# Storing a bf16 part once with a repeating source, and ordering the rows in DRAM by dimension

## The chip, the cores and the metric

The kernel runs on one core of a Trainium2 chip. The metric is the device time of one execution in microseconds (us). A core has TensorE (PE, matrix products and transposes), VectorE (DVE), ScalarE (ACT), GpSimd (POOL) and SyncE (SP, which here only issues DMAs), and 16 DMA engines that move data between DRAM and the on-chip memory.

## The reference, cut to what matters

The input x is 8 batches of 512 rows of 128 numbers. Four layers follow one another, each adding to x: attention a (its weights are sigmoids of sums of sines), a mixture-of-experts layer, attention b (softmax with a relative position term), and the experts again. What the change touches are the two attention layers:

```
x = x + attn_a(layernorm(x));  x = x + ffn(layernorm(x))
x = x + attn_b(layernorm(x));  x = x + ffn(layernorm(x))

q = (x @ Wq.T + bq)   k = (x @ Wk.T + bk)   v = (x @ Wv.T + bv)     # 16 heads of 8 numbers
attn_a: sim = q k / sqrt(8) / temp;  w = sigmoid(sum_f alpha * sin(2 pi sim / freq + phi)); normalised; w v
attn_b: scores = q k / sqrt(8) + q pos + k pos;  softmax;  probs v
```

The products q k are computed from bf16 numbers and must be nearly as exact as in float32. So every q and k is split into three bf16 parts, high (h), middle (m) and low (l), with q = h + m + l. Six of the nine products of a part of q with a part of k are kept.

## The kernel before, in words

The work runs as blocks, one after the other; a block starts when every engine has finished the one before. In order: `project_block("a")`, `wave_attention`, `wave_output`, `layer_norm`, `experts`, `project_block("b")`, `distance_attention`, `layer_norm`, `experts`, `last_block`.

**project_block** (from L160) loops over the 8 batches. DVE normalises x for the batch two ahead (`normalise`, L338); TensorE transposes it (L508); ACT copies it out of PSUM (L464); TensorE makes q, v and k (L518, L520, L522); ACT adds the bias and writes `full` (L472, L477) and its bf16 high part (L481); DVE subtracts that to get `rest` (L359, in layer a after the largest absolute value, L357); ACT casts `rest` to the middle part (L485); DVE subtracts again and writes the low part (L368). All parts are held in two buffers, by the parity of the batch. A part is a tile of 128 partitions (16 heads of 8 dimensions) by 512 rows of x. DVE also adds the bias to v (L347); in layer b the result lies in `Vs`, again two buffers.

SP sends the parts to DRAM in `send(b)`, in program order: for q and then for k it goes through the six letters of LEFT = "hhmhlm" or RIGHT = "hmhlhm" and issues one DMA of 128 KB for each, so each part is stored as many times as its letter stands there. That gives 12 DMAs for a batch; layer b has a 13th, `v_b` (L269). In DRAM the six rows of eight dimensions form NR = 48 rows: row r * 8 + d is part r of dimension d. Matching rows of q and k hold the six kept products, so one matrix product over 48 rows gives q k. In layer a an array is (batch and head, 48, 512) and a DMA writes runs of 1 KB. In layer b it is (48, 4, batch and head, 128): the 512 rows cut into four tiles, and a DMA writes runs of 256 bytes. The same is done once for the position table, `t_parts`, from 8 partitions (L295).

Three kinds of wait tie the engines to the stores: the buffer of a part is written again only when the stores of two batches before have landed (`stored`, in front of L481 and L368), and `Vs` only when `v_b` has (`v_stored`, in front of L347). At the end of the block SP waits for all stores. In layer a, GpSimd ends its part with a maximum over all partitions of the largest values that DVE found (L405, then L448, then L450).

**wave_attention** loads 48 rows of four heads for each group of four heads (L597), runs of 1 KB. Its inner loop is untouched.

**distance_attention** (from L1511) works on two batches (32 heads) at a time. The unit is a pair of a q tile and a k tile of 128 rows; 16 units make a group, there are four groups. `load` (L1678 to L1682) brings one tile of 32 heads into 48 partitions, twice, at partitions 0 and 64 (`ODD`), 384 KB each; in DRAM the 32 heads of a row are 8 KB without a gap. `ks` has three buffers and `qs` two. A k tile is loaded when the last content product (L1808) of the unit that used its buffer is done, a q tile after the last unit of the q tile two before. GpSimd then spreads each loaded tile with four copies of about 2 us (`spread`, L1735) into `kb` or `qb`, and TensorE's position products (L1795) read these in halves. SP, GpSimd, TensorE, ACT and DVE each follow a fixed order that is worked out ahead (`plan`, `dve_plan`, `spread_steps`).

Of the kernel before, what the change touches and what calls it, by code (L numbers as in the profile page):

```python
# [8 lines left out]
BF16 = mybir.dt.bfloat16  # L9
# [6 lines left out]
P = 128  # L16
B, L, D = 8, 512, 128
H, HD = 16, 8
# [16 lines left out]
ACT_LAST = (0,)  # L35


LEFT = "hhmhlm"
RIGHT = "hmhlhm"
NR = len(LEFT) * HD  # L40
ODD = 64
FRAC = 24
# [5 lines left out]
def build(nc, a):  # L48
    ctx = ExitStack()
    with ctx:  # L50
        dram = {
            n: nc.dram_tensor(n, (B * H, NR, L), BF16, kind="Internal").ap()
            for n in ("qa_parts", "ka_parts")
        }
        for n in ("qb_parts", "kb_parts"):
            dram[n] = nc.dram_tensor(n, (NR, QT, B * H, P), BF16, kind="Internal").ap()
        dram["xn"] = nc.dram_tensor("xn", (NT * P, D), F32, kind="Internal").ap()
        dram["ys"] = nc.dram_tensor("ys", (TILES * P, D), F32, kind="Internal").ap()
        dram["t_parts"] = nc.dram_tensor("t_parts", (NR, 2, WIN), BF16, kind="Internal").ap()
# [100 lines left out]
def project_block(nc, sb, ps, sem, layer, a, X, V, ident, mv, rstd, dram, params, bound):  # L160
# [10 lines left out]
    with ExitStack() as c:  # L171
# [64 lines left out]
        t_stored = sem(c, layer + "_t_stored")  # L236
        block = c.enter_context(nc.Block())
        nload = 6 + (3 if wave else 0)
        each = 16 * len(LEFT)

        @block.sync
        def _(sp):
            x = a["x"].rearrange("b (t p) d -> b p t d", p=P)

            def load_x(b):
                sp.dma_start(X[:, b * QT:(b + 1) * QT, :], x[b]).then_inc(x_loaded[b], 16)

            def send(b):
                u = b % 2
                for s, (_, dst, order) in enumerate(sides):  # L250
                    for r, w in enumerate(order):
                        if r == 0:
                            sp.wait_ge(high, b * NS + s + 1)
                        if w == "l":
                            sp.wait_ge(low, b * NS + s + 1)
                        if w == "m":
                            sp.wait_ge(mid, b * NS + s + 1)
                        if wave:
                            sp.dma_start(
                                dram[dst][b * H:(b + 1) * H, r * HD:(r + 1) * HD, :],  # L260
                                part[s, w][:, u, :]).then_inc(stored[s][u], 16)
                        else:
                            sp.dma_start(
                                dram[dst][r * HD:(r + 1) * HD, :, b * H:(b + 1) * H, :]
                                .rearrange("d t h n -> h d t n"),
                                part[s, w][:, u, :].rearrange("p (t n) -> p t n", t=QT)).then_inc(stored[s][u], 16)
                if not wave:
                    sp.wait_ge(v_taken, (b + 1) * QT)
                    sp.dma_start(dram["v_b"][b, :, :],  # L269
                                 Vs[:, u].rearrange("p g t h d -> p (g t h d)")).then_inc(v_stored[u], 16)  # L270

            if wave:
                load_x(0)
                load_x(1)
                sp.dma_start(temp[:, 0:1], a["temperature"].to_broadcast((P, 1))).then_inc(small, 16)
                sp.dma_start(raw[:, 0, :], a["phi"].to_broadcast((P, H * NF))).then_inc(small, 16)
                sp.dma_start(raw[:, 1, :], a["alpha"].to_broadcast((P, H * NF))).then_inc(small, 16)
            for t, src in ((wq, "wq"), (wk, "wk"), (wv, "wv")):
                sp.dma_start(t[:], a[layer + "_" + src]).then_inc(small, 16)
            for t, src in ((bq, "bq"), (bk, "bk")):  # L280
                sp.dma_start(t[:], a[layer + "_" + src]).then_inc(small, 16)
            sp.dma_start(bv[:], a[layer + "_bv"].to_broadcast((P, D))).then_inc(small, 16)
            if wave:
                for b in range(2, B):
                    load_x(b)
                sp.wait_ge(t_clear, 1)
                sp.dma_start(t_full[:, 0, 0:WIN - 1], a["table_up"]).then_inc(t_loaded, 16)
                sp.dma_start(t_full[:, 1, 0:WIN - 1], a["table_down"]).then_inc(t_loaded, 16)
            for b in range(B):
                send(b)  # L290
                if wave and b == B - 2:
                    sp.wait_ge(t_step, 6)
                    for way, order in enumerate((LEFT, RIGHT)):
                        for r, w in enumerate(order):
                            sp.dma_start(dram["t_parts"][r * HD:(r + 1) * HD, way, :],  # L295
                                         t_part[w][:, way, :]).then_inc(t_stored, 16)
            for u in range(2):
                if not wave:
                    sp.wait_ge(v_stored[u], 16 * (B // 2))
                for s in range(NS):  # L300
                    sp.wait_ge(stored[s][u], each * (B // 2))
            if wave:
                sp.wait_ge(t_stored, 32 * len(LEFT))

        @block.vector
        def _(dve):
# [1204 lines left out]
def distance_attention(nc, sb, ps, sem, a, X, ident, dram):  # L1511
# [125 lines left out]
    with ExitStack() as c:  # L1637
# [38 lines left out]
        def _(sp):  # L1676

            def load(dst, src, q, t, landed):  # L1678
                g = q // QT
                for at in (0, ODD):  # L1680
                    sp.dma_start(dst[at:at + NR, :, :],
                                 dram[src][:, t, g * BH:(g + 1) * BH, :]).then_inc(landed, 16)  # L1682

            def load_q(q):
                if q >= 2:
# [327 lines left out]
```

## Time and profile before

| what | value |
|---|---|
| time, median of 3 runs | 4173.84 us (4168.84 to 4179.46) |
| the profiled execution: its own time, its span | 4163.56 us, 4161.8 us |
| project_block a | starts with the program, ends about 113 us |
| wave_attention | about 113 to 2082 us |
| project_block b | about 2521 to 2610 us |
| distance_attention | about 2611 to 3754 us for its loads, to about 3830 in all |
| share of the span: PE, DVE, ACT, POOL | 82%, 83%, 69%, 27% |
| mean share of the 16 DMA engines by queue 1 (SP's DMAs) | 12.3% |

The shares of busy time are means over blocks of very different kinds. The change touches two short blocks and the loads of a long one, so a stretch has to be read by itself.

### The profile page before, as it was taken

To read this page: it belongs to the slowest core of one execution; us is meant where nothing else is said; L and a number is where in the kernel's file an instruction comes from. 1 tells how busy PE (TensorE), PEld (TensorE's weight loads), DVE (VectorE), ACT (ScalarE), POOL (GpSimd) and SP (SyncE) were. 2 spreads that over 40 slices of the span, in tenths; PEclk is the share of its full clock that TensorE was granted. 3 is DMA by queue.
4 is the path that set the end of the run, shared out by engine and by line. 5 is a ranking of instruction groups with operands and counts; after the bars stand their busy time and mean duration, and the time that the engine had idled before them with its cause. 6 is when DMAs were issued, how large, how long until landed. Compare 5 with 4: busy or idle time off the path is not lost. (4 is left out here: it accounts for less than half of the span.)

```text
span 4161.8 us, 71345 instructions
## 1 busy us (share of the span) xinstructions
PE 3403.4 (82%) x27092; PEld 2090.7 (50%) x27092; DVE 3438.3 (83%) x4264; ACT 2880.8 (69%) x2433; POOL 1126.6 (27%) x983
## 2 busy tenths in 40 slices
PE   3799999999999999999938933688988888897990
PEld 2233333333333333333336932587887887887790
DVE  7899999999999999999847634678788787787662
ACT  3799999999999999999804313466665666664530
POOL 2111221121121112112101541535334335321235
PEclk8899999999999999999967966799999999998995
DMA  4100000000000000000032226411202102102122
GB/s 132 30 6 13 13 13 6 13 13 10 9 13 13 6 13 13 13 6 13 5 106 72 68 52 138 81 25 32 45 18 47 31 17 47 30 18 64 34 65 66
DMA packets 145098, 146.44 MB, mean 35 GB/s; under 512 B 62673, under 2 KB 123697, under 8 KB 140113
## 3 DMA queue, kind: packets, MB, share of 16 engines
q1 hardware_dynamic: 136144, 125.04, 12.3%
q0 software_dynamic: 8704, 17.84, 1.8%
q8 instruction: 186, 3.05, 0.3%
q14 instruction: 64, 0.52, 0.0%
HBM read 90.73 MB, written 52.10 MB: 34 GB/s over the span
## 5 line engine op out<-in xcount | busy, mean ns | idle before, releaser
L704 PE MATMUL psA<-wave,diag 128*128 128x512 f32 x3072 | 1433.9, 618 | 138.2 <-DVE score L860 86.7
L772 ACT ACTIVATE wave<-wave 128x2048 f32<-128x2048 int32 x640 | 1180.8, 1904 | 3.3 <-DVE wave L847 2.2
L704 PEld LDWEIGHTS psA<-wave,diag 128*128 128x128 f32 x3072 | 579.8, 195 | 893.2 <-issue 693.6
L641 POOL TENSOR_TENSOR diag<-ident,par 128x128 f32<-128x128 f32 x384 | 298.1, 803 | 1431.2 <-PE psA L704 1431.2
L822 DVE TENSOR_SCALAR wave<-s,par 128x2048 int32<-128x2048 int32 x480 | 610.6, 1272 | 0.0
L847 DVE TENSOR_SCALAR wave<-wave 128x2048 int32<-128x2048 int32 x512 | 608.0, 1211 | 0.0
L1735 POOL COPY kb<-ks 48x1024 bf16<-48x1024 bf16 x160 | 330.7, 2067 | 590.3 <-PE psR L1795 421.9
L1876 ACT COPY r<-psR 128x1024 f32<-128x1024 f32 x320 | 310.7, 1025 | 163.0 <-PE psR L1795 163.0
L737 ACT ACTIVATE s<-psS,par 128x1024 int32<-128x1024 f32 x256 | 282.8, 1105 | 128.8 <-PE psS L667 128.8
L1885 ACT ACTIVATE W<-psR 128x1024 f32<-128x1024 f32 x256 | 253.4, 1025 | 167.7 <-PE psR L1820 164.8
L860 DVE SCALAR_TENSOR_TENSOR score<-wave,par,psA 128x1024 f32<-128x1024 f32 x256 | 317.2, 1268 | 35.0 <-PE psA L704 35.0
L1915 DVE TENSOR_TENSOR S<-psR,S 128x1024 f32<-128x1024 f32 x192 | 234.6, 1222 | 112.9 <-PE psR L1811 112.9
L1930 DVE TENSOR_TENSOR S<-S,m 128x1024 f32<-128x1024 f32 x256 | 324.7, 1319 | 0.6
L860 DVE SCALAR_TENSOR_TENSOR score<-wave,par,score 128x1024 f32<-128x1024 f32 x256 | 316.1, 1272 | 0.0
L1820 PE MATMUL psR<-ident,S 128*128 128x128 f32 x2048 | 263.3, 279 | 53.7 <-DVE S L1930 52.5
L1922 DVE TENSOR_REDUCE mx<-S 128x8 f32<-128x1024 f32 x256 | 303.8, 1213 | 1.7
L1811 PE MATMUL psR<-ident,r 128*128 128x128 f32 x2048 | 282.4, 284 | 0.0
L1876 ACT COPY S<-psR 128x1024 f32<-128x1024 f32 x192 | 188.4, 1018 | 131.5 <-PE psR L1795 131.5
L1820 PEld LDWEIGHTS psR<-ident,S 128*128 128x128 f32 x2048 | 226.5, 142 | 77.1 <-DVE S L1930 71.7
L679 PE MATMUL psO<-score,Vg 128*9 128x512 f32 x1056 | 239.8, 596 | 7.8 <-ACT score L754 7.8
L754 ACT ACTIVATE score<-score 128x2048 f32<-128x2048 f32 x132 | 241.4, 1900 | 6.1 <-DVE score L860 5.7
L1811 PEld LDWEIGHTS psR<-ident,r 128*128 128x128 f32 x2048 | 232.8, 146 | 0.0
(259 smaller groups left out, 4444.0 us busy)
## 6 DMA issues: line engine op xcount, KB each, us to landing
ks<-kb_parts SPq DMA_DIRECT2D x56, 384.0 KB, 6.2
qs<-qb_parts SPq DMA_DIRECT2D x32, 384.0 KB, 6.2
ys<-f_ys SPq DMA_DIRECT2D x36, 256.0 KB, 2.5
wave_out<-og SPq DMA_DIRECT2D x33, 256.0 KB, 2.1
o<-wave_out SPq DMA_DIRECT2D x8, 1024.0 KB, 5.2
qp<-qa_parts SPq DMA_DIRECT2D x32, 192.0 KB, 3.5
kp<-ka_parts SPq DMA_DIRECT2D x32, 192.0 KB, 3.9
f_wu<-in_w_up SPq DMA_DIRECT2D x2, 2048.0 KB, 10.3
```

The lines of the kernel that those rows point to most:

```text
L641: ins = pool.tensor_tensor(diag[:, h % 2, f, :], ident[:], par[:, u, 1, h * NF + f:h * NF + f + 1] .to_broadcast((P, P)), ALU.mult)
L704: mm = pe.matmul(psA[:, kt, :], diag[:, h % 2, f, :], wave[:, h % 2, f, kt * L:(kt + 1) * L], start=(f == 0), stop=(f == PE_F - 1), skip_g ...
L772: act.activation(wave[:, h % 2, f, :], angle[:, h % 2, f, :], ACT.Sin, scale=float(TWO_PI / 2.0 ** 32)).then_inc(sine, 1)
L822: dve.tensor_scalar(angle[:, h % 2, f, :], src, scalar, par[:, u, row, h * NF + f:h * NF + f + 1], ALU.mult, ALU.add).then_inc(turned if f ...
L847: dve.tensor_scalar(angle[:, h % 2, f - 1, :], at, 32 - FRAC, None, ALU.logical_shift_left).then_inc(cut, 1)
L860: dve.scalar_tensor_tensor(out=score[:, u * HG + h, cols], in0=wave[:, h % 2, f, cols], scalar=par[:, u, 1, h * NF + f:h * NF + f + 1], in ...
L1735: pool.tensor_copy(dst[rows, pairs, odd, :], src[rows, :, :].rearrange("r h (n two) -> r n h two", two=2)[:, pairs, :, odd]).then_inc(read ...
L1811: mm = pe.matmul(slot[:, j, :], r1[:, u % 2, k * HB + j, :], ident[:], start=False, stop=True, is_transpose=True, skip_group_check=True)
L1820: mm = pe.matmul(slot[:, i, kt * P:(kt + 1) * P], S[:, 2 * j + i, kt * P:(kt + 1) * P], ident[:], start=(kt == 0), stop=True, is_transpose ...
L1876: act.copy(dst[:, :, k * CP:(k + 1) * CP], psR[:, n % RING, :, :].rearrange("p a (n h) -> p h (a n)", h=BH)).then_inc(act_took, 1)
L1922: dve.tensor_reduce(mx[:, hs, kt], S[:, hs, kt * P:(kt + 1) * P], AX.X, ALU.max).then_inc(maxed, 1)
L1930: dve.tensor_tensor(S[:, hs, :], S[:, hs, :], m[:, hs].rearrange("p (h a) -> p h a", a=1).to_broadcast((P, 2, L)), ALU.subtract).then_inc( ...
```

## The change

Each part is stored once, by a DMA whose source repeats the part (a step of 0 over `count` copies), into all of its rows. For that the six letters are put in another order (LEFT "hhhmml", RIGHT "mhlhmh"; the same six pairs hh, hm, hl, mh, mm, lh), so that the rows of one letter have a constant step, and a row in DRAM is now d * 6 + r. `PLACES` gives for each letter its first row, step and count. A batch has 6 stores in place of 12, of 3, 2 and 1 copies (384, 256 and 128 KB); the bytes are the same. Layer b uses the layout of layer a, (batch and head, 48, 512); its stores write runs of 1 KB, and `load` in distance_attention gathers runs of 256 bytes: 48 rows of 32 heads, 1536 runs where there were 48 of 8 KB.

```diff
-LEFT = "hhmhlm"
-RIGHT = "hmhlhm"
+LEFT = "hhhmml"
+RIGHT = "mhlhmh"
+
+PLACES = {LEFT: (("h", 0, 1, 3), ("m", 3, 1, 2), ("l", 5, 1, 1)), RIGHT: (("h", 1, 2, 3), ("m", 0, 4, 2), ("l", 2, 1, 1))}
...
-            for n in ("qa_parts", "ka_parts")
+            for n in ("qa_parts", "ka_parts", "qb_parts", "kb_parts")
         }
-        for n in ("qb_parts", "kb_parts"):
-            dram[n] = nc.dram_tensor(n, (NR, QT, B * H, P), BF16, kind="Internal").ap()
...
-        each = 16 * len(LEFT)
+        each = 16 * len(PLACES[LEFT])
...
-                    for r, w in enumerate(order):
-                        if r == 0:
-                            sp.wait_ge(high, b * NS + s + 1)
-                        if w == "l":
-                            sp.wait_ge(low, b * NS + s + 1)
-                        if w == "m":
-                            sp.wait_ge(mid, b * NS + s + 1)
-                        if wave:
-                            sp.dma_start(
-                                dram[dst][b * H:(b + 1) * H, r * HD:(r + 1) * HD, :],
-                                part[s, w][:, u, :]).then_inc(stored[s][u], 16)
-                        else:
-                            sp.dma_start(
-                                dram[dst][r * HD:(r + 1) * HD, :, b * H:(b + 1) * H, :]
-                                .rearrange("d t h n -> h d t n"),
-                                part[s, w][:, u, :].rearrange("p (t n) -> p t n", t=QT)).then_inc(stored[s][u], 16)
+                    for w, first, step, count in PLACES[order]:
+                        sp.wait_ge({"h": high, "m": mid, "l": low}[w], b * NS + s + 1)
+                        sp.dma_start(
+                            dram[dst][b * H:(b + 1) * H, :, :].rearrange("h (d r) n -> (h d) r n", d=HD)
+                            [:, first:first + step * (count - 1) + 1:step, :],
+                            part[s, w][:, u, :].rearrange("p (a n) -> p a n", a=1).to_broadcast((P, count, L))
+                        ).then_inc(stored[s][u], 16)
...
-                        for r, w in enumerate(order):
-                            sp.dma_start(dram["t_parts"][r * HD:(r + 1) * HD, way, :],
-                                         t_part[w][:, way, :]).then_inc(t_stored, 16)
+                        for w, first, step, count in PLACES[order]:
+                            sp.dma_start(
+                                dram["t_parts"][:, way, :].rearrange("(d r) n -> d r n", d=HD)
+                                [:, first:first + step * (count - 1) + 1:step, :],
+                                t_part[w][:, way, :].rearrange("p (a n) -> p a n", a=1).to_broadcast((HD, count, WIN))
+                            ).then_inc(t_stored, 16)
...
                     sp.dma_start(dst[at:at + NR, :, :],
-                                 dram[src][:, t, g * BH:(g + 1) * BH, :]).then_inc(landed, 16)
+                                 dram[src][g * BH:(g + 1) * BH, :, t * P:(t + 1) * P]
+                                 .rearrange("h r n -> r h n")).then_inc(landed, 16)
```

## Rows read from the trace of the kernel before

**Rows 1.** The page: busy us of each engine and its share of the span.

```profile
PE 3403.4 (82%) x27092; PEld 2090.7 (50%) x27092; DVE 3438.3 (83%) x4264; ACT 2880.8 (69%) x2433; POOL 1126.6 (27%) x983
```

**Rows 2.** Timeline of SP's issues, project_block a (start, us, instruction), and the next block's first.

```profile
45.31 0.60 SPq L259 DMA_DIRECT2D qa_parts<-a_part0h  x1
...
110.33 0.60 SPq L259 DMA_DIRECT2D ka_parts<-a_part1m  x1
...
113.27 0.35 SPq L597 DMA_DIRECT2D qp<-qa_parts  x1
```

**Rows 3.** Timeline, project_block a: DVE's normalise and low part, ACT's high part.

```profile
53.04 1.10 DVE L338 TENSOR_SCALAR a_xn<-X,mv,rstd 128x128 f32<-128x128 f32 x4
57.22 0.69 DVE L368 TENSOR_TENSOR a_part1l<-a_rest,a_part1m 128x512 bf16<-128x512 f32 x1
58.62 1.10 DVE L338 TENSOR_SCALAR a_xn<-X,mv,rstd 128x128 f32<-128x128 f32 x4
69.78 0.62 ACT L481 CAST a_part1h<-a_full 128x512 bf16<-128x512 f32 x1 [3.98 <-DMA ka_parts<-a_part1m]
```

**Rows 4.** Timeline, the end of project_block a on DVE and POOL.

```profile
95.70 0.69 DVE L368 TENSOR_TENSOR a_part1l<-a_rest,a_part1m 128x512 bf16<-128x512 f32 x1
103.82 0.18 POOL L450 TENSOR_TENSOR bound<-a_topa 128x1 f32<-128x1 f32 x1 [6.84 <-issue]
```

**Rows 5.** Busy time by stretch: PE, PEld, DVE, ACT, POOL, granted clock, DMA share, GB/s.

```profile
52.00:99.00 47.00, 23.11 (x77) 12.95 (x76) 33.83 (x90) 24.38 (x41) 0.37 (x1) 0.80 0.71 198
2546.00:2607.00 61.00, 22.95 (x80) 12.95 (x78) 24.45 (x64) 25.01 (x41) 0.00 (x0) 0.77 0.93 211
2719.00:2726.00 7.00, 5.34 (x131) 4.73 (x128) 3.35 (x3) 5.17 (x6) 0.00 (x0) 1.00 0.59 115
```

**Rows 6.** DMA rate (GB/s in 40 slices), 4153.9 to 4161.5 us: the output's store.

```profile
GB/s 0 0 0 0 0 143 339 348 348 345 350 345 348 345 350 348 353 348 348 350 350 348 345 348 348 345 348 345 353 353 348 348 350 348 350 345 345 116 0 0
```

**Rows 7.** Timeline of SP's issues: six loads of x, each 256 KB in 512 runs.

```profile
6.21 3.91 SPq L246 DMA_DIRECT2D X<-in_x  x6
```

**Rows 8.** Timeline of SP's issues, project_block b, and the next block's first.

```profile
2545.27 0.64 SPq L269 DMA_DIRECT2D v_b<-b_Vs  x1
...
2607.37 0.64 SPq L269 DMA_DIRECT2D v_b<-b_Vs  x1
2612.90 0.80 SPq L1681 DMA_DIRECT2D qs<-qb_parts  x2
```

**Rows 9.** Timeline of DVE, project_block b: a low part, and a later wait for a store.

```profile
2545.24 0.69 DVE L368 TENSOR_TENSOR b_part1l<-b_rest,b_part1m 128x512 bf16<-128x512 f32 x1
2557.02 0.88 DVE L347 TENSOR_TENSOR b_Vs<-b_psV,b_bv 128x128 f32<-128x128 f32 x4 [4.46 <-DMA v_b<-b_Vs]
```

**Rows 10.** The page's DMA issues: size of one, median us from issue to landing.

```profile
v_b<-b_Vs SPq DMA_DIRECT2D x8, 288.0 KB, 2.7
```

**Rows 11.** Timeline, the start of distance_attention: POOL's spreads, and TensorE after the second.

```profile
2619.90 7.82 POOL L1735 COPY qb<-qs 48x1024 bf16<-48x1024 bf16 x4 [5.77 <-DMA qs<-qb_parts]
2627.78 7.89 POOL L1735 COPY kb<-ks 48x1024 bf16<-48x1024 bf16 x4
2631.74 1.73 PEld L1795 LDWEIGHTS psR<-kb,T 112*128 112x128 bf16 x32 [2.09 <-POOL kb L1735]
```

**Rows 12.** Timeline, distance_attention: the spread after a load, the next one, and its reader.

```profile
2796.43 8.12 POOL L1735 COPY kb<-ks 48x1024 bf16<-48x1024 bf16 x4 [11.01 <-DMA ks<-kb_parts]
2810.56 8.24 POOL L1735 COPY qb<-qs 48x1024 bf16<-48x1024 bf16 x4 [6.00 <-PE psR L1795]
2819.86 1.09 PE L1795 MATMUL psR<-qb,T 112*128 112x64 bf16 x32 [0.60 <-DVE S L1915]
3561.22 8.26 POOL L1735 COPY qb<-qs 48x1024 bf16<-48x1024 bf16 x4 [2.19 <-PE psR L1795]
```

**Rows 13.** Timeline of TensorE after ACT's wait in project_block a: first and last product.

```profile
70.93 2.08 PE L518 MATMUL a_psQ<-a_xnT,a_wq 128*128 128x512 f32 x2 [4.64 <-ACT a_xnT L464]
...
74.50 1.92 PE L522 MATMUL a_psK<-a_xnT,a_wk 128*128 128x512 f32 x2
```

More of the change, by code:

```diff
@@ L302, in _ @@
             if wave:
-                sp.wait_ge(t_stored, 32 * len(LEFT))
+                sp.wait_ge(t_stored, 32 * len(PLACES[LEFT]))
         @block.vector
```

## Prediction

> **What bounds the kernel now.** The page's busy times come first [rows 1]: PE and DVE are each busy for four fifths of the span and POOL for a quarter, which says that no DMA bounds the kernel as a whole. The change touches two blocks of some 90 us and the loads of a third, so the rest is read stretch by stretch. The three long blocks (wave attention and the two expert layers) keep their work; only their starting times move.
>
> SP's issues in project_block a show the bound there. From 45.31 to 110.33 us [rows 2] SP issues 92 stores of parts and the 12 small ones of the position table almost without a gap: 0.60 us each, 0.65 from start to start, so a batch of 12 takes 7.8 us (and 92 x 0.65 + 12 x 0.34 = 63.9 of the 65.0 us). No engine is full there [rows 5]: DVE 33.8 of 47 us, PE 23.1, ACT 24.4, DMA 0.71. What the batches are paced by is SP's issuing. ACT then waits for a buffer whose stores haven't landed, 3.98 us in the worst case [rows 3]. Ahead of that, while buffers are free, DVE's `normalise` rows stand 5.58 us apart (53.04 and 58.62 [rows 3]): the pace that compute can keep.
>
> Project_block b is the same with 13 stores: its `v_b` rows stand at 2545.27 and 2607.37, seven batches apart, 8.87 us each [rows 8]. DVE waits 4.46 us for `v_b` to free `Vs` [rows 9], and the DMA engines are 0.93 busy at 211 GB/s [rows 5]: runs of 256 bytes make the engines nearly as full as SP.
>
> **Block a, part by part.** Six stores in place of 12. What does one cost to issue? Bounds: 0.33 us, a `v_b` that comes alone, is below anything seen in a stream; a store now takes 0.65. The six loads of x, each 512 runs over 128 partitions, take 3.91 us, 0.65 each [rows 7]. A repeating store has 128 to 384 runs over the same 128 partitions, so I take 0.65: six are 3.9 us, less than the 5.58 of compute. If issuing costs by the copy instead, 12 copies at 0.65, nothing is gained (a rival below).
>
> The bytes stay: 12 x 131,072 = 1.57 MB a batch. At the rate per busy time that the stream shows, 198 / 0.71 = 279 GB/s [rows 5], they take 5.64 us; at the 348 GB/s of the output's store, a full queue of short runs [rows 6], 4.5 us. Both are at or under compute. So compute sets the pace, 5.58 us a batch, and the position table's six stores saved (0.34 each in the timeline, 2 us) lie in SP's new slack.
>
> Then the end. The last low part of the third batch (b = 2) ends at 57.91 [rows 3]. Three batches at 5.58 bring b = 5 to 74.7. The last two don't normalise, 1.10 us less; I give them 5.0 each for what DVE waits, so 84.7. Now another thing is late: POOL's reduction. The last low part starts at 95.70 and `bound` is done at 104.00 [rows 4], 7.6 us after its end. Today SP is still issuing then, so it costs nothing; afterwards it sets the end: 84.7 + 7.6 = 92.3 us, while the last store lands about 2 + 2.4 us after 84.7. The next block's first row comes 0.5 us after the last landing today (110.33 + 2.4 = 112.7, then 113.27 [rows 2]), so it moves from 113.3 to 92.8: **20.5 us saved**.
>
> **Block b.** Seven issues at 0.65 are 4.6 us, and DVE's own work is 24.45 us in 61, or 3.6 for a batch of 8.87 [rows 5], 4.6 back to back. The bytes are 1.57 + 0.29 = 1.87 MB: 5.4 us at 348 GB/s, 6.7 at 279. A loop adds to it: `v_b` is the last of its batch to be issued and lands 2.7 us later [rows 10], and DVE can't take v two batches on before that. I take 6.0 us, between the two data rates and near the lower, since the queue will be full as it is in [rows 6]. The second batch's last low part ends at 2545.93 [rows 9]; six more batches give 2581.9. Behind it SP still issues three k stores and `v_b` (about 2.5 us), and that lands 2.7 later: 2587.1. Today the last `v_b` lands at 2607.37 + 2.7 = 2610.1 [rows 8]. **23 us saved**; with 5.4 us a batch it would be 26.6, with 6.7 us 18.8.
>
> **The loads of distance_attention.** No row shows a load of 256-byte runs. A pair (both places, 768 KB) keeps the engines busy for 0.59 x 7 = 4.1 us now [rows 5], 21 ns for each future run of 256 bytes if only bytes counted (3072 runs on 16 engines, 192 each). Stores of such runs took 0.93 x 8.87 us less the `v_b` share (about 0.8) for 6144 runs, or 19 ns each. The loads of x took at most 0.65 us for 32 runs of 512 bytes on each engine, or 20 ns each. So 19 ns is the lower end; the upper end is a rival's 64 ns and more. I take 26: a pair then takes 5.0 us, 0.9 more. The issue of one may grow to 2 us at the rate of [rows 7], under the transfer itself.
>
> What covers it: once a q tile, POOL waits for the k tile just loaded, spreads it, and then waits again, 6.0 us, for TensorE to be done with `qb` [rows 12]. The last of these copies ends at 2818.80, and its reader starts at 2819.86. So a pair may land 6.0 + 1.1 = 7 us later (12 times) before TensorE sees it. Three times, where the v of the next group stands in the queue ahead, POOL's wait is only 2.19 (the fourth row of [rows 12]), so 3.2 us. 0.9 us is hidden everywhere but in one place: the start of the block, where q, then k, is loaded with nothing in front. POOL starts when q has landed, and TensorE waits for each of its copies [rows 11]. There it costs **1 us** (by bounds of the bytes alone, 0).
>
> The Trainium skill speaks against this edit: its page "DMA: Bandwidth & Descriptors", section Specifications, says that a transfer needs at least 512 bytes for line rate and that below it the engine does read-modify-write. By that rule, if it doubled the engine time, a pair would take 8.2 us, 4.1 more: hidden 12 times, 0.9 us three times and 4 us at the start, so 7 us in all in place of 1. The same page, section "Why small descriptors are slow", gives 11 cycles for 256 bytes where 8 carry data; that would be an estimated 5.6 us for a pair. The 19 ns of the 256-byte stores, against 58 ns for a run of 1 KB (0.71 x 47 us over 72 stores of 8 runs on each engine), fits the milder rule better.
>
> **Sum.** -20.5 - 23 + 1 = -42.5 us. Against the profiled execution's own 4163.56 us that is 4121.1; the median of the three runs is 10.3 higher, 4173.84, and the forecast for it is **4131 us**.
>
> **Rivals.**
> *The data rate doesn't rise* above 279 GB/s, 0.14: block a loses 1 us of its gain and b 4, with 2 more of waits: -35, 4139. For it: the only rate shown for these stores. Against: the output's store.
> *TensorE's clock*, 0.12. It falls to 1.2 GHz after stalls: the three products of a batch then take from 70.93 to 76.42, 5.5 us [rows 13], and with four transposes about 7.1. The mean granted clock was 0.80 and 0.77 of 2.4 GHz [rows 5]. If it stays low for most of both blocks, 7.1 is the pace: five batches of a lose 1.5 to 2.1 us each (9), six of b 1.1 each (7): -26, 4148. Against: the falls follow stalls of over 4 us, which should go.
> *Issuing costs by the copy, or 198 GB/s is what the memory takes* (1.57 MB at 198 GB/s is 7.9 us, just the batch seen), 0.06: nothing saved, +1 or 2 at the start of distance_attention, 4175. Against: DMA engines 0.71 busy.
> *The 256-byte loads*, 0.08, the case on the other side. Place: POOL's wait for k. With 75 ns a run a pair takes 14.4 us, 10.3 more: 12 x 3.3 + 3 x 7.1 = 61 us, and at the start q and k (four loads, 384 runs on an engine) take 28.8 us from 2612.9 and land 2 later, so k's spread starts near 2643.7 in place of 2627.78, 16 us. 77 - 43.5 = +34: 4208. It decides from 64 ns on: 12 x 1.2 + 3 x 5.0 + 12 = 41. For it: reads of 256 bytes that lie 48 KB apart have no row. Against: the 19 and 20 ns above.
>
> **How the numbers follow.** The forecast has 0.60. This kernel's runs differ by 0.25%, so 0.3%, 12.5 us, is what a measurement tells from no change. The first three cases (0.86) and the mildest form of the last are faster by more: 0.87. Same: 0.06. Slower: 0.07. The range: with 26.6 us in b and 22 in a the gain is 48 us, and the runs of before spread by 5 around the median: 4120. Upward it reaches past the clock rival's 4148 to a partial form of the load's: 4155.
>
> **What would show it.** Project_block a ends near 93 us with `bound` its last row, and SP shows idle time there; 0.65 us between issues in b and its last `v_b` 23 us earlier relative to its start; the DMA share over 0.85 in b; POOL's wait for `ks` up by about 1 us each, with TensorE never waiting for `kb` or `qb` past the start. The prediction is wrong if an issue of three copies takes 1.9 us, if TensorE's granted clock is near 0.5 in both blocks, or if a `ks` load lands later than 13 us after its issue.

## The result, and the profile after

Both kernels ran in turn on one chip, five times each. Before: 4172.34 us median (4168.84 to 4179.46). After: **4114.87 us** (4113.30 to 4123.44). The ratio is 0.9869 (0.9857 to 0.9881). The change is faster by about 1.3%, 57 us in this comparison and 48 to 51 us in two later ones of the same two kernels. The forecast of 4131 us is 16 us too high, and the time lies 5 us under the predicted range.

The profiled execution of after took 4119.65 us (span 4117.9), against 4121.1 forecast for it. So for the execution that the sum was made against it is 1.5 us off, and for the median 16. The small one is luck, as the section on the prediction shows: the terms of the sum were 5.6 us off together, and the profiled execution of after was 4.8 us above its median.

The page's busy times and DMA packets of after, answering [rows 1]. PE, DVE and ACT do the same work; there are 84,431 more packets under 512 bytes (147,104 where 62,673 stood): the loads of `distance_attention` now bring such packets, and the stores of layer b no longer do.

```profile
PE 3405.4 (83%) x27092; PEld 2091.6 (51%) x27092; DVE 3435.6 (83%) x4264; ACT 2880.4 (70%) x2433; POOL 1135.8 (28%) x983
DMA packets 237592, 146.43 MB, mean 36 GB/s; under 512 B 147104, under 2 KB 220416, under 8 KB 236832
```

Timeline of SP's issues in project_block a of after (start, us, instruction), answering [rows 2]. The next block starts at 94.83 in place of 113.27.

```profile
44.85 0.40 SPq L253 DMA_DIRECT2D qa_parts<-a_part0m  x1
...
52.28 0.55 SPq L253 DMA_DIRECT2D ka_parts<-a_part1h  x1
...
56.33 0.37 SPq L253 DMA_DIRECT2D qa_parts<-a_part0m  x1
...
59.12 0.62 SPq L253 DMA_DIRECT2D ka_parts<-a_part1l  x1
...
89.17 0.67 SPq L253 DMA_DIRECT2D ka_parts<-a_part1l  x1
94.83 0.35 SPq L591 DMA_DIRECT2D qp<-qa_parts  x1
```

Timeline of DVE and POOL there, answering [rows 3, 4]: `normalise` rows 5.59 us apart, the last low part, and `bound`, which is now the last row of the block.

```profile
53.35 1.11 DVE L332 TENSOR_SCALAR a_xn<-X,mv,rstd 128x128 f32<-128x128 f32 x4
58.94 1.11 DVE L332 TENSOR_SCALAR a_xn<-X,mv,rstd 128x128 f32<-128x128 f32 x4
...
85.70 0.69 DVE L362 TENSOR_TENSOR a_part1l<-a_rest,a_part1m 128x512 bf16<-128x512 f32 x1
94.34 0.18 POOL L444 TENSOR_TENSOR bound<-a_topa 128x1 f32<-128x1 f32 x1 [7.35 <-issue]
```

Busy time by stretch (PE, PEld, DVE, ACT, POOL, granted clock, DMA share, GB/s): project_block a, project_block b, and a pair of `ks` loads, answering [rows 5]. In b the DMA engines are full and move 347 GB/s, the rate of [rows 6]; the granted clock rose from 0.77 to 0.92.

```profile
46.00:83.00 37.00, 27.19 (x99) 15.16 (x97) 34.41 (x87) 27.51 (x46) 0.00 (x0) 0.90 0.84 283
2535.00:2568.00 33.00, 17.50 (x74) 9.66 (x73) 22.52 (x56) 22.82 (x38) 0.00 (x0) 0.92 1.01 347
2681.00:2689.00 8.00, 5.99 (x147) 5.26 (x143) 4.25 (x4) 5.48 (x7) 1.00 (x1) 1.00 0.64 100
```

Timeline of SP's issues in project_block b, answering [rows 8]: the first, a late and the last `v_b`, and the next block's first load. Seven batches stand between the first and the last, 38.59 us, or 5.5 us each; the last six take 5.4 us each on the mean, where 8.87 stood.

```profile
2528.38 0.67 SPq L260 DMA_DIRECT2D v_b<-b_Vs  x1
...
2561.57 0.58 SPq L260 DMA_DIRECT2D v_b<-b_Vs  x1
...
2563.48 0.97 SPq L253 DMA_DIRECT2D qb_parts<-b_part0l  x1
...
2566.97 0.59 SPq L260 DMA_DIRECT2D v_b<-b_Vs  x1
2572.77 1.07 SPq L1675 DMA_DIRECT2D qs<-qb_parts  x2
```

Timeline of POOL in `distance_attention` of after, answering [rows 11, 12]: the start, and a spread after a load with the one behind it.

```profile
2580.12 7.79 POOL L1730 COPY qb<-qs 48x1024 bf16<-48x1024 bf16 x4 [6.11 <-DMA qs<-qb_parts]
2587.97 7.92 POOL L1730 COPY kb<-ks 48x1024 bf16<-48x1024 bf16 x4
...
2688.00 8.27 POOL L1730 COPY kb<-ks 48x1024 bf16<-48x1024 bf16 x4 [10.89 <-DMA ks<-kb_parts]
2702.25 8.22 POOL L1730 COPY qb<-qs 48x1024 bf16<-48x1024 bf16 x4 [5.98 <-PE psR L1790]
```

POOL's waits are those of [rows 12]: 10.89 for `ks` where 11.01 stood, 5.98 for TensorE where 6.00 stood.

Where the trace gained and lost, by stretches from the first SP row of a block to that of the next (the layer_norm block between wave_output and the experts takes 32.4 in both):

```
                                      before   after   moved
start to wave attention's first load  113.27   94.83   -18.4
wave attention                       1971.58 1973.51    +1.9
wave output                            80.98   81.48    +0.5
first expert layer                    322.82  325.56    +2.7
project_block b                        91.83   64.96   -26.9
distance_attention                   1218.14 1214.56    -3.6
second expert layer                   322.90  322.71    -0.2
```

They sum to -44.0, the difference of the spans (43.9) but for rounding. Three stretches that the change doesn't touch moved by 5.1 together, which is the scatter that the experiments have to see through.

### The profile page after: what moved, and what is told of

Read it like the earlier page. It is cut to its first block and busy times, and to the rows that moved or that the text cites. A ratio compares the mean times of both kernels' runs of the same rounds, so it can differ in the third digit from the quotient of the medians.

```text
span 4117.9 us, 71243 instructions
## 1 busy us (share of the span) xinstructions
PE 3405.4 (83%) x27092; PEld 2091.6 (51%) x27092; DVE 3435.6 (83%) x4264; ACT 2880.4 (70%) x2433; POOL 1135.8 (28%) x983
## 2 busy tenths in 40 slices
DMA packets 237592, 146.43 MB, mean 36 GB/s; under 512 B 147104, under 2 KB 220416, under 8 KB 236832
## 3 DMA queue, kind: packets, MB, share of 16 engines
q1 hardware_dynamic: 228640, 125.03, 12.7%
## 5 line engine op out<-in xcount | busy, mean ns | idle before, releaser
L1910 DVE TENSOR_TENSOR S<-psR,S 128x1024 f32<-128x1024 f32 x192 | 234.6, 1222 | 114.0 <-PE psR L1806 113.8
```

## Experiments

### Both kernels again, and each half alone

`before_again` and `after_again` have no edit. `a_only` keeps the new stores in project_block a and leaves layer b's stores, its array in DRAM and the loads of `distance_attention` as they were; `b_only` does the reverse. The small stores of the position table go with b: `a_only` has 12 of them, `b_only` six.

```
a_only:  -  for w, first, step, count in PLACES[order]:   (all layers)
         +  if wave: (the same)   else: the stores of the kernel before
         -  dram[src][g * BH:(g + 1) * BH, :, t * P:(t + 1) * P].rearrange("h r n -> r h n")
         +  dram[src][:, t, g * BH:(g + 1) * BH, :]
b_only:  +  if not wave: (the new stores)   else: the stores of the kernel before
```

> The kernel before, unchanged. The stretches of the two first traces add up to a gain of 43.9 us, the timed runs to 57. Theory 1: the profiled execution of before was a short one (4163.56 us, under all five timed runs), through TensorE's clock in the long blocks; then this profile is 5 to 15 us longer in wave attention and distance attention, while project_block a (first row of the next block at 113.3 us) and b (91.8 us from its first load to the next block's) stay within 0.5 us. Theory 2: the change gains something in the timed runs that a profile hides; then the profile repeats 4163 us and the timed median stays at 4172.

> The changed kernel, unchanged. Both theories: project_block a ends at 94.8 us and b takes 65.0 us again. Theory 1: the long blocks between differ from the first trace by up to 5 us in either direction, and the timed gain over before is between 44 and 57 us. Theory 2: 57 us again, with a trace whose sum again gives 44.

> Only project_block a stores with a repeating source; the position table is stored by 12 small DMAs as before, layer b is as before. By the stretches: block a ends at 94.8 us, as GpSimd's maximum over the partitions sets its end and not SP's issues (if SP's issues set it, 2 us later for the six small stores more). Time -18.5 us, ratio 0.9956. If the extra 13 us of the timed runs belong to block a: -30 us.

> Only layer b is changed, with its layout, its loads of 256-byte runs and the stores of the position table; block a keeps its 12 stores of a batch. By the stretches: block a ends 2 us earlier than before (six small stores less on SP), block b takes 65.0 in place of 91.8 us, distance attention starts 2 us later and is then the same: -27 us, ratio 0.9935. Together with the kernel that has only a changed it adds to the whole change's ratio within 0.1% if the parts don't touch each other.

Measured, medians and ratios to before: before_again 4169.81 (1.0003, 0.9991 to 1.0015); after_again 4116.82 (0.9880, 0.9860 to 0.9901); a_only 4147.89 (0.9951, 0.9933 to 0.9970); b_only 4136.89 (0.9922, 0.9903 to 0.9940). The product of the two halves is 0.9873: they add, and neither hides the other. In us, out of 4168.05: a 20, b 31, both 51.

The stretches of the five profiles agree with that. The start up to wave attention took 113.3 and 117.7 with the old stores, 113.8 in b_only, and 94.8, 96.2 and 96.5 with the new ones. Much of the scatter lies ahead of the first store, so the cleaner measure is from the first store to the next block: 76.5 and 77.5 old, 57.9 and 57.7 new. This too has its scatter: `a_only` and three later kernels below with the same stores in block a take 57.9 to 59.1. Project_block b took 91.8, 91.8 and 91.4 with the old stores, 65.0, 64.8 and 64.6 with the new ones. The two profiles of the kernel before differ by 3.6 us in their spans (4161.8, 4165.4) and the 17 single times of it in this comparison by 24 (4154.79 to 4178.51): one profile stands for the median only to within several us. Neither theory held as written. The second profile of before was 3.6 us longer, not 5 to 15, and not in wave attention and `distance_attention`, which were 1.0 and 3.2 us shorter, but mainly up to the first store (3.3). The timed gain fell from 57 to 51.

The first expert layer takes either 322.6 or 325.6, in kernels old and new (325.6 in `before_cut` below, 322.6 in `after_beside`), so its +2.7 above isn't shown to be the change's.

### What ends project_block a

POOL's reduction over the partitions is replaced by a copy; the maximum over the partitions is left out.

```
-  pool.partition_all_reduce(topa[:], topr[:], P, bass.bass_isa.ReduceOp.max)
+  pool.tensor_copy(topa[:], topr[:])
```

> The changed kernel; GpSimd copies the largest values instead of taking their maximum over the partitions (so that maximum is left out). Theory: after the change the 7.35 us reduction behind DVE's last value sets the end of block a. Then the end goes to the last store's landing: last issue at 89.2 us in the first trace plus 2.8, so 92.0, and the next block starts near 92.5 in place of 94.8: -2.3 us, relative to the first store of the block. Rival: SP's stores set the end, nothing moves (under 0.5 us).

Timeline of POOL, then of SP, at the end of that block without the reduction (this execution's first store is at 33.00, so its times stand against that).

```profile
82.88 0.18 POOL L442 COPY a_topa<-a_topr 128x2 f32<-128x2 f32 x1 [47.67 <-DVE a_topr L399]
83.14 0.19 POOL L444 TENSOR_TENSOR bound<-a_topa 128x1 f32<-128x1 f32 x1
```

```profile
85.30 0.66 SPq L253 DMA_DIRECT2D ka_parts<-a_part1l  x1
...
89.05 0.35 SPq L591 DMA_DIRECT2D qp<-qa_parts  x1
```

POOL ends 2 us before the last store's issue, so the store ends the block: 56.05 us from first store to next block, against 57.7 to 59.1 in six kernels with the reduction. The reduction does set the end after the change, and without it only 1.6 to 3.0 us are won (2.3 expected), because the last store is right behind. In the time (4119.09, 0.9884, 0.9865 to 0.9903) such an amount can't be seen.

### Row order or fewer instructions

The change does two things to a store: rows in DRAM ordered by dimension, and one instruction for all copies. In these two kernels each copy is again a store of its own, 12 a batch, in the new order. In layer a nothing else about the stores of parts differs from the kernel before but the order of the six letters. In layer b the new array also makes the runs longer, 1 KB in place of 256 bytes, so b_single doesn't separate the order from the length of the runs.

```
-  sp.dma_start(... [:, first:first + step * (count - 1) + 1:step, :], ... .to_broadcast((P, count, L)))
+  for i in range(count):
+      sp.dma_start(... [:, first + step * i, :], part[s, w][:, u, :])
```

In layer b (`b_single`):

> The changed kernel, but in layer b each copy of a part is a store of its own again, 12 of 1 KB runs for a batch and v_b, in the new layout. It parts the number of issues from the size of the runs. Theory (SP's issues bind when there are 13): 8.5 us a batch at 0.65 each, block b 3.1 x 7 = 22 us longer than the changed kernel's 65 us: about 86 to 87 us. Rival (the 256-byte runs bound block b before, the engines being 0.93 busy): the 1 KB runs alone bring it to about 5.4 us a batch, 65 us in all.

In layer a (`a_single`):

> The changed kernel, but in block a each copy of a part is a store of its own, 12 for a batch, in the new row order. The same cut in block b took 0.49 us for an issue where the old order took 0.65 to 0.69. Theory: the issue's price comes from the shape (128 rows on both sides against 16 heads x 8 rows), so 12 take 5.9 us, little over DVE's 5.58: the block, from its first store to the next block's first row, is 58 + 1 to 3 us = 59 to 61 us, where the old order took 76.5. Rival: the merging is what counts, 12 stores at 0.65 again: 74 us or more.

Timeline of SP's issues in b_single, from one `v_b` to the next, and the stretch by engine.

```profile
2541.80 0.45 SPq L266 DMA_DIRECT2D v_b<-b_Vs  x1
2542.29 1.43 SPq L255 DMA_DIRECT2D qb_parts<-b_part0h  x3
2543.76 0.92 SPq L255 DMA_DIRECT2D qb_parts<-b_part0m  x2
2544.72 0.45 SPq L255 DMA_DIRECT2D qb_parts<-b_part0l  x1
...
2548.18 0.45 SPq L266 DMA_DIRECT2D v_b<-b_Vs  x1
```

```profile
2545.00:2580.00 35.00, 18.84 (x60) 10.70 (x60) 19.38 (x49) 18.65 (x31) 0.00 (x0) 0.77 0.85 287
```

Three stores in 1.43 us, 0.49 from start to start (1.47 / 3). The same bytes in the old layout took 0.68 (8.87 / 13 [rows 8]). A batch takes 6.4 us, 13 x 0.49 = 6.4: still bound by issuing, at a lower price. The block takes 72.1 us, so both expectations missed: 86 to 87 for a price of 0.65 that stays, 65 for the runs as the only bound. Of 91.8 - 65.0 = 26.9 us the new layout (order and longer runs) gives 19.7 and the merging 7.2. The time of b_single is 4131.19 (0.9902, 0.9881 to 0.9923), between b's old stores and its new ones.

In a_single the same: its SP rows, and its stretch.

```profile
57.39 0.45 SPq L255 DMA_DIRECT2D ka_parts<-a_part1l  x1
57.88 1.43 SPq L255 DMA_DIRECT2D qa_parts<-a_part0h  x3
...
63.80 1.43 SPq L255 DMA_DIRECT2D qa_parts<-a_part0h  x3
```

```profile
55.00:85.00 30.00, 22.28 (x79) 12.25 (x78) 27.96 (x72) 22.09 (x37) 0.00 (x0) 0.89 0.76 253
```

A batch takes 63.80 - 57.88 = 5.9 us, 12 x 0.49, and from first store to next block 61.5 us (59 to 61 expected): some 15.5 of the 19 us come from the order, 3.7 from the merging (2.4 by the longest of the merged kernels, 59.1). Its time is 4124.86 (0.9903, 0.9888 to 0.9918). Runs and bytes are those of the kernel before, so in block a the lower price is shown to come with the order.

What in the order makes it cheaper is not shown, and it isn't the shape of the instruction alone. `v_b` is the same instruction in every kernel. It takes 0.62 to 0.64 us in the stream of the kernel before (0.33 in the one place where it comes alone), 0.45 in the stream of b_single and 0.58 to 1.01 in after. A low part, one copy of 128 KB in the new order, takes 0.45 in a_single and 0.62 in the stream of after. So what an issue takes depends also on what stands around it in the stream.

### How late may a k load be

Four copies of the same 384 KB from DRAM to DRAM are put ahead of each pair of k loads, which delays the landing; nothing reads what they write.

```
+  for i in range(4):
+      sp.dma_start(dram["scratch"][extras[0]], dram["kb_parts"][g * BH:(g + 1) * BH, :, t * P:(t + 1) * P]
+                   .rearrange("h r n -> r h n")).then_inc(extra_done, 16)
+      extras[0] += 1
```

> The changed kernel with four extra DRAM to DRAM copies of 384 KB in runs of 256 bytes ahead of every k load that waits for TensorE. It makes those loads late by about 10 us (four copies of 96 runs on an engine at 26 ns). By the cover worked out in the prediction (7 us, three times 3.2 us), distance attention grows by 12 x 3 + 3 x 7 = 57 us, and POOL's wait for TensorE ahead of the q spread, 6.0 us in the changed kernel, is gone where the k spread came late. Rival: the loads have far more cover (the copies end early enough anyway), under 5 us; or less, since every k load is late and SP is held up too: over 100 us.

Timeline of SP's issues in this kernel, then of POOL: the spreads of an ordinary step and of one at a group's end.

```profile
2680.40 5.86 SPq L1693 DMA_DIRECT2D scratch<-kb_parts  x4
2686.30 3.36 SPq L1679 DMA_DIRECT2D ks<-kb_parts  x2
```

```profile
2695.28 8.23 POOL L1740 COPY kb<-ks 48x1024 bf16<-48x1024 bf16 x4 [18.73 <-DMA ks<-kb_parts]
2703.56 8.19 POOL L1740 COPY qb<-qs 48x1024 bf16<-48x1024 bf16 x4
...
2922.77 8.23 POOL L1740 COPY kb<-ks 48x1024 bf16<-48x1024 bf16 x4 [19.77 <-DMA ks<-kb_parts]
2931.06 8.89 POOL L1740 COPY qb<-qs 48x1024 bf16<-48x1024 bf16 x4
```

The copies were faster than assumed: k lands 14.9 us after the first issue (2695.28 - 2680.40) in place of 7.0 (2688.00 - 2680.98), 7.9 later and not 10 or more. The block takes 1228.0 us, 12.4 more than the mean of the nine other kernels with the new loads (1215.6, from 1211.4 to 1220.2). An ordinary step between q loads takes 70.4 to 72.6 us, as in those, although the landing is 7.9 us late, and the three pairs of steps around a group's end take 158.24, 156.64 and 157.36 where 153.2 stood on the mean of the nine (151.3 to 153.8): 12.7 us together, so within the scatter all of the 12.4 is lost there. So the cover at the 12 ordinary places is at least 7.9 us, a little more than the 7 worked out, and the shorter cover at the three others is real too: 7.9 - 3.2 = 4.7 each, against 4.2 measured. The time is 4129.94 (0.9906, 0.9887 to 0.9926). The expected 57 us came out too large for two reasons: the delay assumed, and the 12 places, which by a cover of 7 us would have cost some 10 us even at 7.9 and cost nothing.

### The loads of before, cut into shorter runs

Every pair of loads, in the kernel before, becomes eight instructions of eight heads each: runs of 2 KB in place of 8 KB.

```
+  for n in range(0, BH, BH // CUTS):
-      sp.dma_start(dst[at:at + NR, :, :], dram[src][:, t, g * BH:(g + 1) * BH, :])
+      sp.dma_start(dst[at:at + NR, n:n + BH // CUTS, :], dram[src][:, t, g * BH + n:g * BH + n + BH // CUTS, :])
```

> The kernel before, with each load of distance attention cut into four DMAs of runs of 2 KB in place of 8 KB. All three profiles with 8 KB runs have one pause of TensorE with nothing it waits for (released by issue) of 1.7 to 3.6 us, beside the loads ahead of the third group, and none of the seven with 256-byte runs has one over 0.7 us. Theory: TensorE's next instructions come over the same DMA engines and wait behind 8 KB packets; with 2 KB ones the longest such pause is under 1 us and the third step between q loads over a group's end takes 69.4 us, as after the change, in place of 73.5 to 74.8. Rival: it is where the code lies or how long the queue is; then the pause stays.

This follows from a thing seen in the traces: in all three kernels with 8 KB runs TensorE pauses once, beside the loads ahead of the third group, for a wait for which the profile shows no releaser. Timeline of TensorE in the kernel before, in before_again and in a_only, then a stretch of the kernel before 20 us after its pause.

```profile
3226.38 0.60 PE L1795 MATMUL psR<-kb,T 112*128 112x64 bf16 x15 [1.66 <-issue]
```

```profile
3229.41 0.81 PE L1795 MATMUL psR<-kb,T 112*128 112x64 bf16 x15 [3.31 <-issue]
```

```profile
3213.41 0.96 PE L1806 MATMUL psR<-kb,T 112*128 112x64 bf16 x15 [3.58 <-issue]
```

```profile
3246.00:3256.00 10.00, 7.93 (x103) 7.48 (x103) 4.21 (x6) 3.50 (x5) 4.04 (x3) 0.66 0.44 96
```

The granted clock doesn't go clearly with the pause: in the kernel before it is 1.00 in the 20 us from 3226 and 0.66 only in the stretch shown, in the other two 0.83 in the 10 us at the pause's end, and in before_cut, without a pause, 0.90 in one stretch. None of the ten traces with 256-byte runs has the pause, nor has before_cut, whose longest wait of the kind is 0.7 us (waits of `psR`'s weight loads: sum in us, count, longest), and its block takes 1208.1 us, the shortest of all.

```profile
PEld psR L1797 <- issue: 28.3, 93, 0.7
```

The two steps between q loads around the second group's end take 157.3 to 158.9 us in the three kernels with 8 KB runs, 153.0 to 153.8 in the nine with 256-byte runs and 152.2 in before_cut; the second of the two alone, for which 69.4 us was expected, takes 65.9. The time is 4163.50 against 4167.40 (0.9989, 0.9979 to 0.9998): some us faster at most. So the pause and 4 to 5 us at that place go with 8 KB runs, and shorter runs without any new order remove them too. That this is why `distance_attention` as a whole didn't get slower is only argued. That TensorE's instruction fetch waits behind 8 KB packets is an argument only; no row shows the fetch.

### The position table's work moved out of project_block a

In all kernels so far eight `normalise` operations of DVE, ahead of the first store, take 18.1 to 19.9 us (14.2 in the kernel without the reduction, where one more of them got done ahead of POOL's work). Timeline of DVE there, in after.

```profile
15.01 18.12 DVE L332 TENSOR_SCALAR a_xn<-X,mv,rstd 128x128 f32<-128x128 f32 x8
```

Beside them POOL splits the position table into parts, six operations over 8 partitions, which in after end at 20.89, 22.84, 26.98, 28.92, 33.04 and 34.99 us. TensorE's transposes, each waiting for a `normalise`, start at 21.03, 22.98, 27.12, 29.06 and 33.18: DVE's operations end one by one with POOL's. The new version does this work, its loads and its stores in wave_output's block, about 1.9 ms later and still ahead of its reader.

```
-  pool.tensor_scalar(t_full ...); pool.tensor_copy(t_part["h"] ...); pool.tensor_tensor(t_rest ...)  # ... six in all
   (the same lines, with t_full, t_rest, t_part and six stores, now in wave_output)
```

> The changed kernel with the preparation of the position table on GpSimd (19 us of work), its two loads and its six stores moved from block a into the wave_output block, where GpSimd has nothing to do. In the first trace DVE's eight normalise instructions take 18.1 us there while the same eight take 2.1 us in block b, and each ends with one of GpSimd's. Theory: GpSimd's table work holds DVE up; then the first store goes out at 21 us in place of 36.9, and the whole kernel gains about 16 us (4100). Rival: DVE waits there for something else (x's loads), no change; or wave_output, where DVE is busy 57 of 110 us, grows by as much as is gained.

> The kernel with the position table prepared in wave_output, beside the changed kernel on the same chip. The traces say 15.8 us less up to the first store, 2 us more in wave_output: 0.9966 of the changed kernel's time, 4103 against 4116 us.

> The changed kernel unchanged, as the reference for the run before it: 4115 us, ratio to before 0.987 to 0.988.

Timeline of DVE, then of SP, in the first of these runs.

```profile
15.13 2.14 DVE L316 TENSOR_SCALAR a_xn<-X,mv,rstd 128x128 f32<-128x128 f32 x8
```

```profile
21.14 0.38 SPq L251 DMA_DIRECT2D qa_parts<-a_part0h  x1
...
80.36 0.35 SPq L562 DMA_DIRECT2D qp<-qa_parts  x1
```

The same eight operations take 2.14 us; the first store goes out at 21.14 (21.00 in the second run) and not at 36.8 to 40.1 (33.0 without the reduction), and wave attention starts at 80.36 and 78.51, 14.5 to 19 us earlier than in the three profiles of the changed kernel. Wave output pays 2 us (83.56 and 84.03, against 81.48). The times are 4104.83 (0.9844, 0.9825 to 0.9862) and 4102.08 (0.9845, 0.9832 to 0.9859), with after_beside, on the same chip as the second, at 4119.47 (0.9888, 0.9873 to 0.9903). This version beats both kernels, the changed one by 17 us beside it on one chip (10 to 15 by the ratios of the first run). The move takes POOL's work and the table's loads and stores out of the block together; that POOL's work is what held DVE up rests on the ends listed above.

## Why the prediction was nearly right, and where it failed

**What bounds the blocks before: right.** SP's issuing did, and for block a this is shown: with the price of an issue lowered and nothing else (a_single), a batch fell to the new price times the count. For block b it is in part argued. b_single fell to price times count too, but its runs are longer, and the engines were 0.93 busy before. What speaks for issuing is that nearly every issue there took 0.62 to 0.66 us, where in after, with the bytes as the bound, they vary from 0.45 to 1.02.

**The price of an issue: right for a wrong reason.** The step took 0.65 us for a merged store from the loads of x [rows 7] and took an issue's price for a property of the instruction. Merged stores take mostly 0.34 to 0.69 us in a, up to 1.02 in b, where the queue is full, so 0.65 was a fair value for a stream of them. But most of the gain (15.5 of 19 us in a, 19.7 of 27 in b) needed no merging, only the new order in a, and the new order with longer runs in b. The rival "issuing costs by the copy" is refuted in both forms: neither the copies nor 198 GB/s were a bound.

**Block a: right in mechanism, 1 to 2 us too high.** Pace 5.59 us (5.58 forecast), end set by `bound` (shown by the kernel without the reduction), next block's start 94.83 against 92.8. The last low part ended at 86.39 in place of 84.7, and the reduction took 8.1 us behind it in place of 7.6. 18.6 to 19.9 us saved against 20.5 by these four profiles, 17.4 at the least with the later ones.

**Block b: the mis-sized term.** Bytes bind, as predicted: DMA share 1.01, above the 0.85 named as its sign. But I took 6.0 us a batch, between the two data rates, where the row of the output's store [rows 6] held to the letter: 347 GB/s, 5.4 us a batch. Six batches at 5.4 are 32.5 us and not 36; that is 3.5 of the 3.9 us by which -26.9 exceeds -23. The lower bound in the text, 26.6, was the value. The loop over `v_b`, a reason for the 6.0, added nothing to the bytes: DVE's longest wait for it fell from 5.4 us (the 4.46 of [rows 9] is not the longest) to 1.8.

Waits in project_block b of after (total us, count, longest):

```profile
DVE b_Vs L341 <- DMA v_b<-b_Vs: 4.0, 4, 1.8
```

**The loads of `distance_attention`: the price right, the sum 3 us off.** A pair keeps the engines busy for 0.64 x 8 = 5.1 us (5.0 forecast), 27 ns for a run of 256 bytes. One of the bounds behind the forecast was misread: the 3.91 us of [rows 7] are SP's issues of the loads of x, not their transfer, so they give no upper bound of 20 ns for a run. From 10 to 12 us the engines moved those loads at 303 GB/s, 27 ns for a run of 512 bytes. The Trainium skill's rule that transfers under 512 bytes fall from line rate by read-modify-write ("DMA: Bandwidth & Descriptors", Specifications) agrees in direction: a pair took 5.1 us where 8 KB runs took 4.1. The doubling to 8.2, the prediction's own assumption, isn't borne out. The estimate of 5.6 us by the Trainium skill's 11 cycles for 256 bytes (same page, "Why small descriptors are slow") lies nearer. The wait for `ks` was to grow by 1 us each; it went from 160.9 us in 15 waits to 176.5 in 16, 0.3 each, and over all kernels the two ranges overlap (10.7 to 10.9 us each in three old, 10.5 to 11.1 in nine new). At the start I foresaw 1 us. The third q load, which waits for work on the first, goes out 81.6 to 82.0 us after the block's first load in the three kernels with 8 KB runs; in the nine with the new loads it is 83.6 to 85.4 in five and 81.4 to 81.6 in four. So the start costs some 2 us or more in some executions and nothing in others; why isn't traced. The block as a whole was 2 us shorter on the mean (1215.6 over nine profiles, 1217.5 over three), 3 us from the +1 forecast, but single profiles of either kind spread by 4 to 9 us, so even its sign isn't certain. What the forecast left out is the pause told of above, with its 4 to 5 us, which went away. Nothing in the profile of before had been read for it, though its row was there.

**Which steps failed.** Two, and they leave more than half of the 16 us open. The first is the sum's terms: block b's 6.0 us a batch, which measured 5.4 (3.9 us), and the +1 for `distance_attention`, which measured -2 (3 us); block a's term was 1.3 us the other way. With the measured sizes the steps come to -19.2 - 26.9 - 2.0 = -48.1, against -42.5: 5.6 us of the 16. (The later profiles of block a would make that 0.6 less.)

The second is the base, the median of 3 runs, 10.3 us above the profiled execution. It was taken as known to a few us, and it wasn't: the median of before was 4172.34 in the first comparison and 4168.05 and 4167.40 in two later ones, so 4173.84 was 1.5, 5.8 and 6.4 us high. Passing from the profile to a median was right in itself; that of before did lie 4 to 9 us above its first profile.

What is left is 9.0 us in the first comparison, 2.8 and -0.5 in the two later ones. The timed gains of the same two kernels were 57.5, 51.2 and 47.9 us, with 43.9 between the two first profiles. The 48.1 from the stretches fits the last of these and lies within their scatter, so the 9.0 are most likely a chance of the first comparison. No stretch shows them, and the cause stays open.

**The rivals.** The data rate did rise. TensorE's clock rose to 0.90 and 0.92 in the two stretches, so a low clock paced nothing; in b_single a batch fell to 6.4 us with the clock still at 0.77. The 256-byte loads cost 27 ns a run, far under the 64 ns from which they decide. No rival took place. The range was too narrow below because it paired the lowest bound of block b with a base known no better than 6 us.

## What to carry to other kernels

When a stream of small stores is bound by the issuing engine, try the order of the rows in DRAM before counting instructions: the same bytes, with 128 rows in SBUF meeting 128 rows in DRAM, issued a quarter faster (0.49 against 0.65 us), and the new layout alone gave three quarters of this gain, in block b with longer runs as a part of it. For a queue that will be full, take the rate of a row where a queue is full, not a middle value. And before a range is set, see how far single executions spread: here the gain of the same change came out between 47.9 and 57.5 us in three comparisons, a spread larger than the error of all terms together.

## What the runs showed of the hardware that was not expected

- An issue by SP of a 128 KB store costs 0.49 us with rows ordered by dimension and 0.65 with the old order; 384 KB from a repeating source costs 0.55 to 0.69 in block a of after. The same `v_b` takes 0.33 alone, 0.62 to 0.64 in the old stream and 0.45 in that of b_single.
- Reading a source row two or three times by a zero step costs the transfer nothing: 347 GB/s at a DMA share of 1.01.
- Loads in 8 KB runs go with one TensorE pause of 1.7 to 3.6 us, in three traces of three; with 2 KB or 256-byte runs it was in none of eleven. The cause isn't shown.
- Eight DVE operations that take 2.14 us alone took 14.2 to 19.9 us beside POOL's work on only 8 partitions. Moving that work was worth 17 us beside the changed kernel, a third as much as the whole change.
- A delay of 7.9 us in each k load cost nothing at 12 places of 15, and 4.2 us at each of the other three.
